# Recurrent attention block with experts: norm chain in six steps, MLP from the seventh, head sums on TensorE

## The reference

```python
xn = layernorm(x)
# attention side
a = rmsnorm(xn, ln1_w); q, k, v, g = a@Wq, a@Wk*s, a@Wv, a@Wg + bg
gk = log_sigmoid(a@Wkg1@Wkg2 + bkg2) / 16
S = S*exp(gk_t)[..., None] + k_t[..., None]*v_t[..., None, :]   # scan over 512 tokens
o_t = q_t . S                                    # 16 heads, k 8 and v 16 wide
o = (o - mean)/sqrt(var + 1e-5) per head;  x1 = xn + (silu(g)*o)@Wo
s = x1 + (silu(rmsnorm(x1, ln2_w)@W1) * (...@W3)) @ W2          # hidden 704
# expert side: 16 experts, hidden 224, top 4 of a softmax router
f = sum over the 4 chosen experts of w_e * (silu(xn@gate_e)*(xn@up_e)) @ down_e
out = x + s * silu(f)
```

## Time and profile before

| | us |
|---|---|
| median of 3 runs | 538.33 (538.22 to 539.1) |
| the profiled execution's own time | 537.45 |
| its span in the trace | 535.7 |
| busy TensorE | 436.6 (82%) |
| busy VectorE | 311.2 (58%) |
| busy ScalarE | 232.7 (43%) |
| busy GpSimd | 291.9 (54%) |

### The profile page before, as it was taken

One profiled execution on the slowest core, in us unless ns is written; L12 is line 12 of the kernel. 1 busy time (PEld: TensorE's weight loads), 2 busy tenths in 40 slices (PEclk: granted clock), 3 DMA queues, 4 the chain that ended last, 5 costly groups with the idle time before them and its releaser, 6 DMA issues.

```text
span 535.7 us, 8820 instructions
## 1 busy us (share of the span) xinstructions
PE 436.6 (82%) x2181; PEld 258.6 (48%) x2182; DVE 311.2 (58%) x593; ACT 232.7 (43%) x527; POOL 291.9 (54%) x221
## 2 busy tenths in 40 slices
PE   3879863164978988895899989999999999999835
PEld 2333320031325434542654657767767767777512
DVE  5887779986998699754556533333333333333226
ACT  3657743002412231313435446556556556655502
POOL 5338883315888888887000026656666656666610
PEclk9999985575989998999799999999999999999969
DMA  8755689755444453439749156766666666664487
GB/s 246 246 186 185 235 315 339 295 167 218 158 155 152 142 183 114 141 103 359 274 131 262 50 168 107 118 105 110 110 108 109 114 101 108 115 107 55 53 245 252
DMA packets 73417, 90.30 MB, mean 169 GB/s; under 512 B 7752, under 2 KB 56488, under 8 KB 73384
## 3 DMA queue, kind: packets, MB, share of 16 engines
q1 hardware_dynamic: 53848, 66.05, 38.9%
q0 software_dynamic: 14448, 19.34, 21.7%
q10 hardware_dynamic: 5088, 4.50, 2.7%
HBM read 50.66 MB, written 39.21 MB: 168 GB/s over the span
## 4 chain that ended last, share of the span: by engine, by line
PE 51%; DVE 17%; POOL 10%; issue 9%; DMA 7%; ACT 3%; another core or an unknown queue 2%; SPq 0%; DVEq 0%; POOLq 0%; ACTq 0%
PE mm_ps L322 28%; PE sum_ps L322 12%; POOL qs L574 5%; DVE st L1041 4%; POOL rows_scratch L609 4%; PE turn_ps L1365 3%; PE mm_ps L1472 3%; DVE kv L1033 3%; DMA vrep<-v_scratch 3%; DMA y_scratch<-y,X 2%; PE mm_ps L1511 1%; PE sum_ps L1343 1%; DMA xn<-in_L_attn_x_dram 1%; DVE anT L986 1%
## 5 line engine op out<-in xcount | busy, mean ns | idle before, releaser
L643 POOL DMA_INDIRECT y_scratch<-y,X x79 | 123.0, 1557 | 135.6 <-ACT y L877 109.0
L574 POOL TENSOR_TENSOR qs<-st,q_sb 128x1024 f32<-128x1024 f32 x32 | 75.6, 2361 | 53.5 <-DVE st L1041 45.3
L322 PE MATMUL mm_ps<-w_gu,xT 128*128 x474 | 102.6, 352 | 1.6 <-DVEq L1251 1.6
L1169 DVE TENSOR_TENSOR xT<-turn_ps,xT 128x256 f16<-128x256 f32 x79 | 33.4, 424 | 87.3 <-ACT xT L788 79.3
L322 PE MATMUL mm_ps<-an2T,w 128*128 128x512 f16 x264 | 66.8, 409 | 18.9 <-issue 6.8
L322 PE MATMUL sum_ps<-wd,hT 112*128 x316 | 81.3, 380 | 0.0
L1041 DVE TENSOR_TENSOR_SCAN st<-sum_ps,kv 128x512 f32<-128x512 f32 x64 | 75.3, 1211 | 1.1
L609 POOL DMA_INDIRECT rows_scratch<-rows,slot_u x64 | 63.2, 988 | 16.8 <-issue 14.1
L322 PEld LDWEIGHTS mm_ps<-w_gu,xT 128*128 128x128 f16 x474 | 46.0, 97 | 32.7 <-issue 2.9
L1343 PE MATMUL sum_ps<-qs,sumk 128*32 128x512 f32 x128 | 37.5, 676 | 29.5 <-POOL qs L574 29.5
L1256 DVE SCALAR_TENSOR_TENSOR h<-mm_ps,X,sl 128x224 f32<-128x224 f32 x79 | 35.6, 451 | 40.1 <-ACT sl L861 36.2
(11 more groups left out here) (184 smaller groups left out, 509.8 us busy)
## 6 DMA issues: line engine op xcount, KB each, us to landing
vrep<-v_scratch SPq DMA_DIRECT2D x64, 256.0 KB
rows_scratch<-zrow SPq DMA_DIRECT2D x20, 548.0 KB, 7.5
X<-rows_scratch SPq DMA_DIRECT2D x80, 137.0 KB, 2.6
w_gu<-y_scratch SPq DMA_DIRECT2D x16, 256.0 KB, 4.5
y_scratch<-zrow ACTq DMA_DIRECT2D x6, 640.0 KB, 7.4
w_gu<-in_L_ffn_gate_proj_dram SPq DMA_DIRECT2D x16, 224.0 KB, 5.6
w_gu<-in_L_ffn_up_proj_dram SPq DMA_DIRECT2D x16, 224.0 KB, 5.9
wd<-in_L_ffn_down_proj_dram SPq DMA_DIRECT2D x1, 3136.0 KB, 16.5
```

The costliest lines, as they stand in the source:

```text
L322: last = nc.tensor.matmul(out_ap, lhsT, rhs, start=(n == 0), stop=(n == len(pairs) - 1))
L574: nc.gpsimd.tensor_tensor(qs[:, u % 2, :, :], st[:, u % 2, :, :], pair_bc(q_sb[:, TOK(a)]), ALU.mult).then_inc(s["qs_ready"], 1)
L643: nc.gpsimd.indirect_dma_start(y_dram[u % 2], bass.IndirectOffsetOnAxis(ap=X[:, u, TOKEN_C:TOKEN_C + 1].bitcast(U32), axis=0), y[:, u, :], ...
L1169: nc.vector.tensor_tensor(xT[:, u % 2, 1, :, :].rearrange("p c n -> p (c n)"), PS[u % 2][:, 0:KC * P], xT[:, u % 2, 0, :, :].rearrange("p ...
```

## The change

- The norm chain takes steps u = 0 to 5, and its split's low half u = 6. MLP_FROM goes from 7 to 6, so there are 38 steps instead of 39, and turn 5 has six.
- The squares are taken from `oT` and `O0` as they are, at the end of `value_half`, before they are turned round. Eight small matmuls of TensorE sum them per head into `HEAD_SUMS` (in `T0`); ScalarE copies 128x64 numbers; VectorE's reduction is gone, its root chain is in u = 0. Turning `oT` round now waits for that copy, since it shares the bank.
- The MLP's m = 0 is issued on TensorE and ScalarE at the end of its step, and `gated(c, 0)` on VectorE a step later, behind that step's recurrence.
- `LAST_SCATTERS` gives turn 3 14 scatters instead of 24, so that turn 4, where GpSimd has no recurrence, issues 20 instead of 10. Turn 2 keeps 24 in another order.
- SyncE issues a pair of experts' loads only when the pair before has landed.
- `experts_at` packs the last six experts in three steps (before, the last four in two).

```diff
@@ -205 +205 @@
-sq = sb("sq", [P, TPB, D], F32, att)
+sq = sb("sq", [P, KC, L], F32, att)
@@ -240,0 +241 @@
+HEAD_SUMS = T0[:, 0:TPB * H]
@@ -250 +251 @@
-    k_bank a_bank kv_ready st_ready qs_ready gla_used oT_evac pool_turn act_turn tpo_ready sq_ready
+    head_sums sums_out k_bank a_bank kv_ready st_ready qs_ready gla_used oT_evac pool_turn act_turn tpo_ready sq_ready
@@ -329,2 +330,3 @@
-HEAD_STEPS = 2 + ROOT_STEPS
-SCATTERS = (1, 4, 3, 3, 4, 3, 3, 3)
+HEAD_STEPS = 1 + ROOT_STEPS
+SCATTERS = (4, 3, 3, 4, 2, 3, 3, 2)
+LAST_SCATTERS = (3, 2, 2, 3, 2, 1, 1, 0)
@@ -349 +351 @@
-MLP_FROM = U - 1
+MLP_FROM = U - 2
@@ -381,0 +384,2 @@
+ALONE = 2 * (U + MLP_FROM - 1) - E
+
@@ -384 +388 @@
-    if n <= E - 4:
+    if n <= ALONE:
@@ -386 +390 @@
-    return (2 * n - E + 2, 2 * n - E + 3)
+    return (2 * n - ALONE - 2, 2 * n - ALONE - 1)
@@ -483,0 +488,2 @@
+        if e % 2 == 0 and e > 0:
+            sp.wait_ge(raw_in[e // 2 - 1], 64)
@@ -617 +623 @@
-            if b and u == 2:
+            if b and u == 1:
@@ -619 +625 @@
-            if u == 5:
+            if u == 4:
@@ -628 +634 @@
-            scatter(SCATTERS[u])
+            scatter((LAST_SCATTERS if a == B - 1 else SCATTERS)[u])
@@ -739,0 +746,3 @@
+        if half:
+            act.wait_ge(s["oT_evac"], a * 2 + 3)
+            nc.scalar.activation(sq[:, 0, :], oT[:, 0, :], ACT.Square).then_inc(s["sq_ready"], 1)
@@ -741,0 +751,2 @@
+        if half:
+            nc.scalar.activation(sq[:, 1, :], O0, ACT.Square).then_inc(s["sq_ready"], 1)
@@ -801 +812,5 @@
-        if c is not None and m < NF:
+        if b is not None and u == 0:
+            wait(act, s["on_ready"], b * 2)
+            act.wait_ge(s["head_sums"], b + 1)
+            nc.scalar.activation(ghead[0][:, :], HEAD_SUMS, ACT.Copy).then_inc(s["sums_out"], 1)
+        if c is not None and 0 < m < NF:
@@ -805,7 +819,0 @@
-                wait(act, s["on_ready"], b * 2)
-                for i in range(2):
-                    act.wait_ge(s["tpo_ready"], b * 2 + (i + 1))
-                    nc.scalar.activation(
-                        sq[:, 2 * i:2 * i + 2, :].rearrange("p t (h d) -> p t d h", d=HD),
-                        PS[i].rearrange("p (t d h) -> p t d h", t=2, d=HD), ACT.Square).then_inc(s["sq_ready"], 1)
-            if u == 1:
@@ -823 +831 @@
-            if u == 6:
+            if u == 5:
@@ -832 +840 @@
-        if b is not None and u == 6:
+        if b is not None and u == 5:
@@ -837,0 +846,2 @@
+        if c is not None and m == 0:
+            gate_silu(c, m)
@@ -1196,0 +1207,7 @@
+        if c is not None and m == 1:
+            gated(c, 0)
+        if b is not None and u == 6:
+            for i in range(KC):
+                dve.wait_ge(s["an2hi_ready"], b * KC + (i + 1))
+                nc.vector.tensor_tensor(an2T[:, 1, i, :], PS[i], an2T[:, 0, i, :],
+                                        ALU.subtract).then_inc(s["an2lo_ready"], 1)
@@ -1204 +1221 @@
-            if u == 1:
+            if u == 0:
@@ -1206,4 +1223,3 @@
-                dve.wait_ge(s["sq_ready"], b * 2 + 2)
-                chain(nc.vector.tensor_reduce(ghead[0][:, :], sq[:, :, :].rearrange("p t (h d) -> p (t h) d", d=HD),
-                                              AX.X, ALU.add))
-                chain(nc.vector.tensor_scalar(ghead[0][:, :], ghead[0][:, :], -0.5 / HD, -0.5 * EPS, ALU.mult, ALU.add))
+                dve.wait_ge(s["sums_out"], b + 1)
+                chain(nc.vector.tensor_scalar(ghead[0][:, :], ghead[0][:, :], -0.5 / (HD * KS), -0.5 * EPS, ALU.mult,
+                                              ALU.add))
@@ -1211 +1227 @@
-            if u == 2:
+            if u == 1:
@@ -1212,0 +1229 @@
+                    dve.wait_ge(s["tpo_ready"], b * 2 + (i + 1))
@@ -1229,5 +1245,0 @@
-            if u == 6:
-                for i in range(KC):
-                    dve.wait_ge(s["an2hi_ready"], b * KC + (i + 1))
-                    nc.vector.tensor_tensor(an2T[:, 1, i, :], PS[i], an2T[:, 0, i, :],
-                                            ALU.subtract).then_inc(s["an2lo_ready"], 1)
@@ -1237 +1249 @@
-        if b is not None and u == 3:
+        if b is not None and u == 2:
@@ -1406 +1418,9 @@
-        if c is not None and m < NF:
+        if b is not None and u == 0:
+            wait(pe, s["an2lo_ready"], b * KC)
+            pe.wait_ge(s["sq_ready"], b * 2 + 2)
+            for t in range(TPB):
+                for kc in range(KC):
+                    last = nc.tensor.matmul(HEAD_SUMS[:, t * H:(t + 1) * H], sq[:, kc, t * P:(t + 1) * P],
+                                            sumk[:, P - H:P], start=(kc == 0), stop=(kc == KC - 1))
+            last.then_inc(s["head_sums"], 1)
+        if c is not None and 0 < m < NF:
@@ -1412 +1432 @@
-                wait(pe, s["an2lo_ready"], b * KC)
+                pe.wait_ge(s["sums_out"], b + 1)
@@ -1422 +1442 @@
-            if u == 3:
+            if u == 2:
@@ -1428 +1448 @@
-            if u == 4:
+            if u == 3:
@@ -1446,0 +1467,2 @@
+        if c is not None and m == 0:
+            gate_up_mlp(c, m)
```

More of the change, by code:

```diff
@@ L1203, in step_fn @@
                 if b is not None:
-                    if u == 1:
-                        chain = sem_chain(dve, s["head_dve"], 0, HEAD_STEPS, b)
-                        dve.wait_ge(s["sq_ready"], b * 2 + 2)
-                        chain(nc.vector.tensor_reduce(ghead[0][:, :], sq[:, :, :].rearrange("p t (h d) -> p (t h) d", d=HD),
-                                                      AX.X, ALU.add))
-                        chain(nc.vector.tensor_scalar(ghead[0][:, :], ghead[0][:, :], -0.5 / HD, -0.5 * EPS, ALU.mult, ALU.add))
-                        chain(rsqrt_of_neg_half(chain, ghead[1][:, :], ghead[0][:, :], ghead[2][:, :]))
-                    if u == 2:
+                    if u == 0:
+                        chain = sem_chain(dve, s["head_dve"], 0, HEAD_STEPS, b)
+                        dve.wait_ge(s["sums_out"], b + 1)
+                        chain(nc.vector.tensor_scalar(ghead[0][:, :], ghead[0][:, :], -0.5 / (HD * KS), -0.5 * EPS, ALU.mult,
+                                                      ALU.add))
+                        chain(rsqrt_of_neg_half(chain, ghead[1][:, :], ghead[0][:, :], ghead[2][:, :]))
+                    if u == 1:
                         for i in range(2):
+                            dve.wait_ge(s["tpo_ready"], b * 2 + (i + 1))
                             nc.vector.tensor_tensor(
```

## The result

The changed kernel took 543.49 us in the median of 7 runs (541.82 to 544.82), the kernel before 539.46 beside it: 1.0067 of its time, 95% interval 1.0042 to 1.0091. It is slower, by four microseconds, where I had forecast twelve less, and outside my range. The profiled execution took 544.12 us (span 542.4); the two profiled executions lie 6.7 us apart, the medians 4.0.

The account below looks back on a forecast made before the run. GpSimd was taken to pace turns 2 and 3, and a TensorE stall tied to the weight-load burst to hold turn 4. Terms 0 - 3.2 - 2.75 + 1.7 - 8.5 + 0.8 + 0 = -11.95 us gave 526.4 us, range 521 to 533.5.

Parts of the forecast that it names:

- The stall, -8.5: Turn 4: thinning the burst of weight loads to pairs removes most of TensorE's stall, -8.5 us (0 to 10.3 off).
- the stall stays: Rival: turn 4's stall remains since its cause isn't seen, giving 534.9 us; chance 0.15.
- Turn 3, -3.2: Turn 3: ten scatters less on GpSimd shorten the turn by 3.2 us (0 to 6).
- my walk: Turn 3: new engine orders followed with profiled durations, giving 43.9 us from first product to last read-out, against 47.6.
- Head sums and squares, +1.7: Turn 4: squaring the last read-out and eight small matmuls on TensorE add 1.7 us (1.0 to 2.6).
- Turns 1 and 2, 0: Turns 1 and 2: lost reduction and moved MLP work net 0, from -1.2 to +2.75 us.
- Turn 4's 12 matmuls, -2.75: Turn 4: TensorE enters with 12 more matmuls already done, -2.75 us.
- the last splits, +0.8: End of turn 4: six experts instead of five left to split after the last `gated`, +0.8 us (0 to 2.2).
- The loads behind the pairs, 0: X and `wd` loads: at 4.9 us a pair, `wd` arrives at 297, before TensorE asks at 299; cost 0.
- the pairs come too slowly: Rival: slow pair landings delay `wd`, making the kernel slower, 541.1 us at 7.3 us a pair; chance 0.06.

Follow-up runs that it names:

- a1: The kernel before, unchanged, run again with a trace on chip 13: 530.9 us.
- a2: The changed kernel, as it is, run again on chip 13: 531.99 us, 1.0032 of the kernel before there.
- e1: The changed kernel without SyncE's wait for a pair of loads, 14 and 20 scatters kept, on chip 7: 543.03 us, ratio 1.0073 to the kernel before.
- e5: The changed kernel with experts' loads started only after all 64 scatters landed and splits from n = 6 on, on chip 9: 555.84 us, total not comparable.
- b1: The changed kernel with SyncE waiting for the pair before the last, on chip 0: 545.61 us, ratio 1.0092 to the kernel before.
- e3: The changed kernel with 24 and 10 scatters again and no pair wait, on chip 7: 536.51 us, ratio 0.9934 to the kernel before.
- e2: The changed kernel with 24 and 10 scatters again, pair wait kept, on chip 7: 535.38 us, ratio 0.9949 to the kernel before.
- e12: The changed kernel with 24 and 10 scatters, last ten paced, two pairs in flight, head sums behind product m = 2, chip 11: 527.08 us, 0.9925 of the kernel before.
- e8: The changed kernel with its last 20 scatters replaced by plain writes of the same bytes, on chip 9: 536.01 us, ratio 0.9939 to the kernel before.
- a4: The same kernel as e12, run on chip 13: 527.29 us, ratio 0.9918 to the kernel before.

## Why the prediction was wrong

**The stall, -8.5.** This is the step that failed. The first expert's product, which I had put near 297.5, came at 315.32, beyond the 306 that was to mean that the stall stayed. I named the burst of loads as its cause, because the DMA share of 0.95 and the late signal stood side by side; the scatters stood beside it too, and I priced ten more of them behind the last product at nothing. From the last read-out to the Wo product it is 24.3 us before against 15.7 in a1, so the stall was worth 8.6 us, as I had estimated; the size was right and its cause wrong. After it is 31.3 against 13.5 in a2: 17.8 us. Instead of taking 8.5 away the change added 9.2. The end of the run of scatters and the end of the stall moved together in eight traces (e1 to e5, b1 and both kernels, 1.5 to 6.2 us apart), and without the pair wait and with it, moving ten scatters alone moved the time by 7.5 and 6.4 us (e1 to e3, the changed kernel to e2). None of my rivals had this; the rival "the stall stays" had the right place and no growth.

**Turn 3, -3.2.** 46.8 us from first product to last read-out, where my walk gave 43.9; a2 gives exactly 43.9 (188.74 to 232.66), against 47.3 in a1. The order of the walk was right, the clock was not in it; and that a2 hits its number to a tenth is in part luck, since a2's product behind the sums took 4.44 us, 1.7 more than the walk's 2.75. In the changed kernel the sums and the product behind them took 3.56 + 4.82 us, in a2 1.93 + 4.44, and from GpSimd's first product to the turning of `oT` it is 8.3 us (188.51 to 196.84) against 5.5 (188.74 to 194.22): all of the difference. The idle time at the turn's start, the new wait for the squares in it, is what TensorE did before the clock fell; the granted clock from 186 to 197 us is 0.53 in the changed kernel, 0.84 in a2 and 1.00 in e12, which takes that wait away. How much is lost behind the same two gaps differs from run to run: a2's sums still ran at 2.4 GHz (1.93 us). VectorE's add waits for TensorE ahead of the last scans as I had written, 1.7 us.

**Head sums and squares, +1.7.** They cost 0.79 + 1.93 = 2.7 at 2.4 GHz, just above my upper bound. Eight matmuls of 16 columns are 16 records and take 1.93 us, 0.12 a record; the eight turns are 8 records in 1.04, 0.13 a record. So the sums run at the turns' rate, with two records to each matmul. My 2.0 came near by luck: I took the 24 records of a W2 step for 24 matmuls, but the kernel issues 12 there (the description above has 24 as well), so eight of them take 4.0.

**Turns 1 and 2, 0.** They gained 1.8 us, and 2.3 on chip 13, more than my best case of 1.2; what gained it I did not follow. Without the stall my terms add up to -3.45 us at the first expert; on chip 13 it was -7.2, these 2.3 and 1.1 more in turn 4, so that part of the sum was short by half.

**Turn 4's 12 matmuls, -2.75, and the last splits, +0.8.** On chip 13 the stretch to the Wo product shortens by 2.2 us. The 12 matmuls and the head sums cancel there (-2.75 + 2.7), where I had a gain of 1.05; the gain is one that I had not booked. In a1 TensorE waits 0.58 us for `h_mlp` and 1.36 for `gs`, 1.9 together, and in a2, with the chain and the gating in their new places, TensorE has neither wait. The stretch behind the Wo product grows by 0.7 us there and 1.4 in the changed kernel, inside my 0 to 2.2.

**The loads behind the pairs, 0.** In the changed kernel a pair took 5.9 to 6.6 us beside the scatters (the first from 235.33 to 241.46) and 5.3 to 6.0 behind them, not 4.9; X went out at 278.8, not 271. Behind the stall nobody noticed. Without it the rival "the pairs come too slowly" is what happens: in a2 a pair takes 5.9 us on average, X goes out at 276.2 and `wd` is there at 302.4, 26.2 us later, as I had it. The wait of 6.84 us is near the 7 that I had named for pairs of 6.2 us, but the agreement is luck: pairs of 5.9 give 5 by my sum, and TensorE asked at 295.6, 3.4 us sooner than the 299 that I had reckoned with. There the change comes out 0.3% slower, by the rival's mechanism and not by the stall.

So on the three chips with the stall one of my terms was the wrong way round, and on the other two a second one, priced at 0, cancelled the rest. Why a run of scatters holds TensorE's signals up on chips 0, 7 and 9 and not on 11 and 13 stays open; the 20 scatters start over 24.1 us in the changed kernel and 24.2 in a2, and from 237 to 257 us the DMA engines move 324 GB/s before against 319 in a1, and 266 against 254 in a2. Nor is the way by which scatters hold a signal up shown by any run.

## What to carry to other kernels

When a stall stands beside two things at once, move each of them alone before the removal of one is booked as a gain; the price of the other one, if it is moved the wrong way, is as large. A wait that thins a queue has a deadline behind it: work out when the last load in the row is asked for in the case where everything else goes well. And put work ahead of a small dependent step at a turn's start, so that TensorE doesn't stand before it.

## What was unexpected of the hardware

- The kernel before takes 539 to 540 us on chips 0, 7 and 9, and 531 on 11 and 13, with nothing changed. The difference is the stall, 8.6 us between the traces; whether it belongs to the chip or to the occasion isn't shown.
- On the first group, beside a run of GpSimd's scatters ScalarE waits up to 21.7 us (e1) for a signal of TensorE, and 10.7 us with no load beside them (e5). With plain writes of the same bytes there is no such wait (e8), but 20 of them are issued in 10.75 us, 0.54 each against 1.27 for a scatter, and so they were over at 242.8.
- After gaps of 1.93 and 0.79 us TensorE ran the head sums at 1.2 GHz in the changed kernel (3.56 us) and most of the product behind them (4.82 where 2.75 is possible). After gaps of the same lengths in a2 the sums took 1.93 us, at 2.4, and the product 4.44. With the second gap closed it stayed at 2.4 in e12, but in a4, the same kernel on another chip, the first product still took 3.76.
